# Eight-head edge attention: residual and bias accumulated, centred, in the output product's bank, and a new order of the steps

## The reference, cut to what matters

```
residual = x
q = (x @ Wq + bq).reshape(n, H, HD)
k = (x @ Wk + bk).reshape(n, H, HD)
v = (x @ Wv + bv).reshape(n, H, HD)
score = jnp.einsum('ehd,ehd->eh', q[dst], k[src]) / math.sqrt(HD)
score = score + edge_attr @ We + be
m = jax.ops.segment_max(score, dst, num_segments=n)
exp_s = jnp.exp(score - m[dst])
ssum = jax.ops.segment_sum(exp_s, dst, num_segments=n)
attn = exp_s / (ssum[dst] + 1e-08)
out = jax.ops.segment_sum(attn[..., None] * v[src], dst, num_segments=n)
out = out.reshape(n, D) @ Wo + bo
h = out + residual
mu = h.mean(-1, keepdims=True)
var = ((h - mu) ** 2).mean(-1, keepdims=True)
return (h - mu) / jnp.sqrt(var + 1e-05) * gamma + beta
```

## Time and profile before

| | us |
|---|---|
| median of 3 runs (4201.67 to 4219.3) | 4212.16 |
| the profiled execution | 4234.81 |
| its span | 4233.1 |
| third layer's stage in it | about 2,885 to 3,631 |

### The profile page before, as it was taken

One profiled execution on the slowest core, in us unless ns is written; L12 is line 12 of the kernel. 1 busy time (PEld: TensorE's weight loads), 2 busy tenths in 40 slices (PEclk: granted clock), 3 DMA queues, 4 the chain that ended last, 5 costly groups with the idle time before them and its releaser, 6 DMA issues. The chain is left out here.

```text
span 4233.1 us, 48032 instructions
## 1 busy us (share of the span) xinstructions
PE 2727.4 (64%) x11826; PEld 1768.2 (42%) x11826; DVE 3385.3 (80%) x7569; ACT 2542.3 (60%) x5535; POOL 2439.2 (58%) x2202
## 2 busy tenths in 40 slices
PE   2777877888870588845444553442888787577774
PEld 1555555555550244425433442341444444244442
DVE  2688999999997788837765774883999999699886
ACT  1677777778872366635553562442777777465554
POOL 5455555566630566436636646755566662587777
PEclk7999899999995677756766765565899999566555
DMA  3377567566652888727765764662233332333332
GB/s 87 120 176 182 172 188 193 178 201 193 194 181 74 236 254 254 224 90 225 237 202 167 235 215 140 196 193 74 66 85 85 85 85 60 87 97 97 94 95 68
DMA packets 402066, 644.05 MB, mean 152 GB/s; under 512 B 127455, under 2 KB 207720, under 8 KB 401790
## 3 DMA queue, kind: packets, MB, share of 16 engines
q1 hardware_dynamic: 332030, 527.96, 41.0%
q0 software_dynamic: 69760, 113.02, 11.0%
HBM read 347.78 MB, written 296.81 MB: 152 GB/s over the span
## 5 line engine op out<-in xcount | busy, mean ns | idle before, releaser
L1603 POOL DMA_INDIRECT gs_g<-table_xw,slot_idx x588 | 614.6, 1045 | 454.4 <-issue 250.1
L896 POOL DMA_INDIRECT gs_t<-table_x,slot_idx x392 | 435.1, 1110 | 370.1 <-POOLq L83 144.4
L505 POOL DMA_INDIRECT gs<-x,src_idx x200 | 215.9, 1079 | 406.4 <-DMA xd_rows<-gd 319.6
L378 PE MATMUL ps<-ident,own_g 128*128 128x128 f32 x588 | 145.8, 395 | 466.5 <-DVE own_g L1705 383.3
L1649 ACT ACTIVATE hT_g<-u_g 128x512 f32<-128x512 f32 x147 | 92.5, 630 | 516.5 <-DVE u_g L1717 340.9
L1710 DVE TENSOR_TENSOR_SCAN agg_g<-same_seg,agg_g,ps 128x512 f32<-128x512 uint8 x147 | 187.8, 1278 | 228.7 <-DMA table_x<-x_b 104.3
L1272 POOL DMA_INDIRECT slot_idx<-node_map,src_idx x200 | 239.5, 1198 | 196.6 <-DMA slot_idx<-node_map,src_idx 92.9
L378 PEld LDWEIGHTS ps<-ident,own_g 128*128 128x128 f32 x588 | 97.9, 200 | 507.3 <-DVE own_g L1705 415.9
L505 POOL DMA_INDIRECT gd<-x,dst_idx x200 | 245.2, 1226 | 60.9 <-issue 60.3
L1879 POOL DMA_INDIRECT out<-x_t,end_idx x196 | 232.8, 1188 | 65.0 <-issue 58.8
L896 POOL DMA_INDIRECT own_t<-table_x,own_idx x196 | 225.6, 1151 | 59.7 <-issue 59.7
(11 more groups left out here) (366 smaller groups left out, 9479.7 us busy)
## 6 DMA issues: line engine op xcount, KB each, us to landing
table_xw<-xw_b SPq DMA_DIRECT2D x147, 512.0 KB
table_x<-x_b SPq DMA_DIRECT2D x98, 512.0 KB
own_g<-table_xw SPq DMA_DIRECT2D x147, 256.0 KB
x_in<-x SPq DMA_DIRECT2D x49, 512.0 KB
y_g<-table_x SPq DMA_DIRECT2D x49, 512.0 KB
table_xw<-xw_g SPq DMA_DIRECT2D x98, 256.0 KB
out<-y_g SPq DMA_DIRECT2D x49, 512.0 KB
pen_t<-pen_row SPq DMA_DIRECT2D x98, 256.0 KB
```

The costliest lines, as they stand in the source:

```text
L378: last = nc.tensor.transpose(to[0:width, j * P:(j + 1) * P], t[:, j * width:(j + 1) * width], ident[:])
L505: pool.indirect_dma_start(out=to[k % 3][:, j * D:(j + 1) * D], out_offset=None, in_=x, in_offset=bass.IndirectOffsetOnAxis(ap=of[:, n:n + ...
L896: pool.indirect_dma_start(out=self.B[L % RING][g][:, t * D:(t + 1) * D], out_offset=None, in_=table, in_offset=bass.IndirectOffsetOnAxis(a ...
L1603: pool.indirect_dma_start(out=gs[c % 6][:, j * D:(j + 1) * D], out_offset=None, in_=tables[layer], in_offset=bass.IndirectOffsetOnAxis(ap= ...
```

## The change

The new h is made in PSUM. `copy_xT` adds bo to each column of `xdT` while it copies (`bo_col`), so that `xdT` holds the own rows plus bo, turned. `rows_o` first multiplies those by `centre` (the identity minus 1/128), which turns them back into rows and takes their mean away, and then accumulates the products with Wo on top in the same bank. Wo itself is centred once at the start of the program, so K[7] holds h minus its mean. `xo`, `h_res` and the shift `nm` of the normalisation "d" go. `d.stats` reads K[7] in place of `u`, and `d.apply` reads K[7] and only scales. So K[7] is now held until `d.apply` has finished: `rows_o` of lane L waits for it of lane L-1. As Wq is now multiplied with rows that have bo in them, Wq times bo is taken off bq at the start. All places of the stage's plan are new. The number of table loads stays.

```
-                "load": (1, "ea_in pen_in"), "residual": (129, "xo x2b"),
-                "turn_x": (-37, "xsT_ps xdT_ps"), "copy_xT": (62, "xsT xdT"), "products": (78, "k_ps q_ps"),
...
+                "load": (1, "ea_in pen_in"), "residual": (152, "x2b"),
+                "turn_x": (-58, "xsT_ps xdT_ps"), "copy_xT": (17, "xsT xdT"), "products": (42, "k_ps q_ps"),
...
+                nc.tensor.matmul(ps[:, 5, P:P + 1], Wq[:], bo_col[:], start=True, stop=True).then_inc(S("bo_q_ps"), 1)
...
+                V.tensor_reduce(wo_sum[:], Wo[:], AX.X, ALU.add).then_inc(S("wo_sum"), 1)
+                v.wait_ge(S("wo_sum"), 1)
+                V.scalar_tensor_tensor(out=Wo[:], in0=wo_sum[:, 0:1].to_broadcast([P, D]), scalar=-1.0 / D, in1=Wo[:],
+                                       op0=ALU.mult, op1=ALU.add).then_inc(S("wo_c"), 1)
...
+                V.tensor_tensor(bq[:], bq[:], ps[:, 5, P:P + 1], ALU.subtract)
...
                         @step("rows_o")
                         def _(L):
+                            b = B[L % RING]
+                            step.due(pe, "d_out", L, 1)
+                            step.due(pe, "xdT", L)
+                            for j in range(SUB):
+                                nc.tensor.matmul(K[7][:, j * D:(j + 1) * D], b["xdT"][:, j * P:(j + 1) * P], centre[:],
+                                                 start=j == 0, stop=False, skip_group_check=True)
                             step.due(pe, "oT", L)
-                            step.due(pe, "h_res", L, 1)
-                            rows_times(pe, K[7], B[L % RING]["xsT"], Wo).then_inc(S("wo_ps"), 1)
+                            for j in range(SUB):
+                                last = nc.tensor.matmul(K[7][:, j * D:(j + 1) * D], b["xsT"][:, j * P:(j + 1) * P], Wo[:],
+                                                        start=False, stop=j == SUB - 1, skip_group_check=True)
+                            last.then_inc(S("wo_ps"), 1)
...
-                            nc.scalar.copy(b["xdT"][:], K[1]).then_inc(S("xdT"), 1)
+                            nc.scalar.activation(b["xdT"][:], K[1], ACT.Identity, bias=bo_col[:, 0:1]).then_inc(S("xdT"), 1)
...
+                        @step("d.apply")
+                        def _(L):
+                            b = B[L % RING]
+                            step.due(act, "d_rs", L)
+                            for j in range(SUB):
+                                last = nc.scalar.activation(b["v"][:, j * D:(j + 1) * D], K[7][:, j * D:(j + 1) * D], ACT.Copy, scale=b["rs"][:, j:j + 1])
+                            last.then_inc(S("d_out"), 1)
...
-                            V.tensor_tensor(rows4(b["xo"][:]), rows4(b["own"][:]), each_row(bo), ALU.add).then_inc(S("xo"), 1)
...
+                        @step("d.stats")
+                        def _(L):
+                            ln_stats(v, step, "d", L, B[L % RING], K[7], "wo_ps")
+
+                        @step("d.scale")
                         def _(L):
                             b = B[L % RING]
-                            step.due(v, "wo_ps", L)
-                            step.due(v, "xo", L)
-                            V.tensor_tensor(b["u"][:], K[7], b["xo"][:], ALU.add).then_inc(S("h_res"), 1)
-
-                        ln_vector(v, step, B, "d", "u", "h_res")
+                            step.due(v, "d_sd", L)
+                            nc.vector.reciprocal(b["rs"][:], b["sd"][:]).then_inc(S("d_rs"), 1)
```

More of the change, by code:

```diff
@@ L115, in build @@
     Wq, Wk, Wv, Wo = (sb(n, [P, D]) for n in ("Wq", "Wk", "Wv", "Wo"))
-    bq, bk, bv = (sb(n, [P, 1]) for n in ("bq", "bk", "bv"))
+    bq, bk, bv, bo_col = (sb(n, [P, 1]) for n in ("bq", "bk", "bv", "bo_col"))
     bo, gamma2, beta2 = (sb(n, [P, D]) for n in ("bo", "gamma2", "beta2"))
@@ L157, in build @@
         sums = tb("sums", [P, 6, 4])
-        bo_sum = tb("bo_sum", [P, 1])
+        bo_sum, wo_sum = tb("bo_sum", [P, 1]), tb("wo_sum", [P, 1])
         Win, WinT, Ws0 = tb("Win", [P, D]), tb("WinT", [P, D]), tb("Ws0", [P, D])
@@ L1771, in build @@
             lag, plan = HOP4_LAG, {
-                "load": (1, "ea_in pen_in"), "residual": (129, "xo x2b"),
-                "turn_x": (-37, "xsT_ps xdT_ps"), "copy_xT": (62, "xsT xdT"), "products": (78, "k_ps q_ps"),
-                "values": (173, "v_ps"), "copy_z": (73, "kb"), "qk": (118, "qk"), "scores": (81, "z_ps"),
-                "maximum": (157, "M_first M dz Dm0 Dm"), "gather": (-420, ""), "exps": (172, "p F"),
-                "sums": (192, "msg den num"), "scores_e": (54, ""), "turn_sums": (218, "den_rows"), "divisor": (276, "dn rd"),
-                "widen_rd": (264, "rd_wide"), "turn_rd": (260, "rdT_ps"), "divide": (303, "oT"), "rows_o": (339, "wo_ps"), "h_res": (330, "h_res"),
-                **ln_plan("d", 400, 358, 425, 437), "x3_pre": (437, "dg x3_pre"), **ln_plan("e", 467, 483, 502, 509),
-                "store": (565, "stored"), "turn_q": (581, "x3T_ps"), "copy_q": (632, "x3T"),
-                "query": (648, "q3_ps"), "keep_q": (649, "q_kept"), "store_q": (655, "q_out")}
+                "load": (1, "ea_in pen_in"), "residual": (152, "x2b"),
+                "turn_x": (-58, "xsT_ps xdT_ps"), "copy_xT": (17, "xsT xdT"), "products": (42, "k_ps q_ps"),
+                "values": (126, "v_ps"), "copy_z": (74, "kb"), "qk": (111, "qk"), "scores": (72, "z_ps"),
+                "maximum": (186, "M_first M dz Dm0 Dm"), "gather": (-420, ""), "exps": (156, "p F"),
+                "sums": (224, "msg den num"), "scores_e": (13, ""), "turn_sums": (197, "den_rows"), "divisor": (311, "dn rd"),
+                "widen_rd": (290, "rd_wide"), "turn_rd": (263, "rdT_ps"), "divide": (324, "oT"), "rows_o": (284, "wo_ps"),
+                **ln_plan("d", 343, 359, 397, 370), "x3_pre": (465, "dg x3_pre"), **ln_plan("e", 472, 479, 580, 594),
+                "store": (640, "stored"), "turn_q": (602, "x3T_ps"), "copy_q": (638, "x3T"),
+                "query": (672, "q3_ps"), "keep_q": (695, "q_kept"), "store_q": (700, "q_out")}
         else:
@@ L1790, in build @@
         with ExitStack() as tmp:
-            hop = Line(tmp, f"t{kind}", plan, lag, "xsT pen kb qk p F den num msg xo " + ("xdT w" if kind == 2 else "own u x4"),
+            hop = Line(tmp, f"t{kind}", plan, lag, "xsT pen kb qk p F den num msg " + ("xdT w" if kind == 2 else "xo own u x4"),
                       {"gs": (table, NT + GT, slot_idx), **({"own": (table, NT + GT, own_idx)} if kind == 2 else {})})
@@ L1867, in _ @@
                     def _(L):
-                        for name in ["xsT_ps"] + ["xdT_ps", "xo", "x2b"] * (kind == 2):
+                        for name in ["xsT_ps"] + ["xdT_ps", "x2b"] * (kind == 2):
                             step.due(pool, name, L, RING)
@@ L2034, in _ @@
                             nc.scalar.copy(B[L % RING]["q"][:], K[6][0:4, :]).then_inc(S("q_kept"), 1)
-                        ln_act(act, step, B, "d", "v", "u")
+                        @step("d.root")
+                        def _(L):
+                            ln_root(act, step, "d", L, B[L % RING])
+                        @step("d.apply")
[5 more added lines that the diff above has]
+                            last.then_inc(S("d_out"), 1)
                         ln_act(act, step, B, "e", "xn", "u")
@@ L2130, in _ @@
                             hop.due_gathered(v, L)
-                            V.tensor_tensor(rows4(b["xo"][:]), rows4(b["own"][:]), each_row(bo), ALU.add).then_inc(S("xo"), 1)
                             V.tensor_tensor(rows4(b["w"][:]), rows4(b["own"][:]), each_row(beta2), ALU.add).then_inc(S("x2b"), 1)
-                        @step("h_res")
+                        @step("d.stats")
+                        def _(L):
+                            ln_stats(v, step, "d", L, B[L % RING], K[7], "wo_ps")
+                        @step("d.scale")
                         def _(L):
                             b = B[L % RING]
-                            step.due(v, "wo_ps", L)
-                            step.due(v, "xo", L)
-                            V.tensor_tensor(b["u"][:], K[7], b["xo"][:], ALU.add).then_inc(S("h_res"), 1)
-                        ln_vector(v, step, B, "d", "u", "h_res")
+                            step.due(v, "d_sd", L)
+                            nc.vector.reciprocal(b["rs"][:], b["sd"][:]).then_inc(S("d_rs"), 1)
                         @step("x3_pre")
```

3 lines of the change are left out of this document (2 added, 1 removed).

## The result

The changed kernel takes **4259.3 us** (median of 4 runs, 4258.19 to 4261.95), the kernel before, beside it, 4213.15 (4 runs). The ratio is 1.0121, interval [1.0094, 1.0148]: slower by 46 us, where 32 us less were forecast. The changed kernel's profiled execution took 4261.95 us, that of the kernel before 4234.81: 27 more.

The account below looks back on a forecast made before the run. DVE bound the kernel at 13.38 us a lane; after the change a circle through ACT and PE would, at 12.5 plus 0.2 for the clock. 47 lanes save 32 us: 4212.2 - 32 = 4180, range 4147 to 4222.

Parts of the forecast that it names:

- DVE's own work: DVE's instructions in a lane: `xo`, `h_res` and `nm` go, 0.11 us comes in, 12.0 us if DVE never waits.
- The circle through ACT and PE: From ACT's `kb` to the next lane's `kb`: 12.5 us a lane; as likeliest outcome 4161 to 4191 us, chance 0.50.
- the one from 12.5 to 12.7: Allowance in the lane time for PE's low clock lengthening `scores`, `turn_x` and `query`: 0.2 us a lane.
- the clock: PE's low-clock share halves to 9%, 1.1 us a lane, a third to a half on `scores`, `turn_x`, `query`: 0.2 us.
- Rival D: PE's clock drops on `scores`, `turn_x` and `query` in each lane: 14.2 us a lane, 38 us more, 4250; chance 0.10.
- The argument against D: PE's remaining idle time is 1 to 1.5 us a lane, where it was 3.6.
- C: DVE's `d.stats` and maximum scan wait for PE: 12.93 to 13.8 us a lane, 4191 to 4232 us; chance 0.18.
- The sum: Whole kernel: 47 x (13.38 - 12.7) = 32 us less, start and drain cancelling, giving 4180 us.

Follow-up runs that it names:

- the third chip: Chip that ran the new arithmetic at the old places, alone (3858.98 us, ratio 0.9804 to the kernel before) and with instructions added at the start of the stage's code.
- i1: Changed kernel with a one-row transfer in place of each indirect gather from lane 10 (counted from 0) on: 4147.0 us, ratio 0.9849 to the kernel before.
- e3: Changed kernel with only `query` moved, ahead of the next lane's `turn_x` on PE: 4246.08 us, ratio 0.9979 to the kernel before.
- i2: Changed kernel without the four products with `centre`, all places kept: 4201.03 us, ratio 0.9966 to the kernel before.
- e5: Changed kernel with `d.stats` moved later on DVE, behind the divisor's steps: 4254.63 us, ratio 1.0064 to the kernel before.
- h0: Changed kernel, unaltered, run again on the fourth chip: 4270.02 us, ratio 1.0096 to the kernel before.

## Why the prediction was wrong

- **DVE's own work: right, 0.25 too high.** 12.0 us a lane; 11.75 measured on the third chip with DVE busy throughout. BN_STATS on PSUM 416 ns (median of 70), on SBUF 425 in the same lanes: no cost, so the Trainium skill's 120 fixed cycles for a source in PSUM ("VectorE: DVE Perf Modes", on the TRN2 errata) are again not to be seen.
- **The circle through ACT and PE: right.** 12.5 forecast, 12.2 measured wherever nothing disturbs it (the lane of 12.17, i1 from lane 6 on), and 11.9 where e3 takes `turn_x` out of it. `d.apply` took 1.14 us for four passes (1.1 to 1.3 forecast). At the old places it is shorter and DVE binds, 11.75.
- **The step that failed** is the one from 12.5 to 12.7, in the words "I take half of today's share ... 0.2 us": everything that could hold PE up was priced at 0.2 us a lane. Measured are 1.9 over the undisturbed 12.2, from two things.
- **One is the clock, mis-sized.** The low clock did not halve as PE's idle time shrank: PEclk is 0.92 against 0.91, 2.15 us at the lower level in a lane (2.4 before). Nor does a third to a half of it fall on the circle's steps: 75% falls on `scores`, `turn_x` and `query`. At half speed, 2.15 us can cost at most 1.1 of the 1.9; the 18 lanes without a late result are 1.1 longer than 12.2.
- **The other was put at nothing: late results.** The prediction read PE's rows as completions. The 28 lanes with late results hold some 70 of the 89 us that the 46 lanes take over 12.17 each, part of it by the clock drops in them. They could have been seen: the kernel before has 28 such results. There they cost nothing (13.35 us in lanes with one, 13.52 in the others), which fits its 3.6 us of idle PE in a lane.
- **Rival D's price (14.2 us a lane, 4250 us; measured 14.1 and 4259) was met in part by luck.** Its mechanism, the drop on `scores`, `turn_x` and `query`, is real, and pure in i2: 1.7 forecast, 1.8 measured (13.95 against 12.17). But it comes in some lanes and not in each, and late results, which D does not have, make up the rest. The argument against D was that PE's idle time would be 1 to 1.5 us. It is 1.7 in an undisturbed lane, and it doesn't decide: lanes with the same idle time do and don't have a drop. What does decide stays open.
- **C, waits for PE at `d.stats`: real, but small.** 33.6 us in 10 + 11 waits over 35 lanes, two thirds of it (the `remote` ones) behind late results. e5 brings it from 46 us in h0's window of 500 us to 11 and gains 0.5 us a lane; in its place DVE waits 34 us for `kb`.
- **The sum holds where nothing disturbs**: lanes of 12.2 give 47 x 1.2 = 56 us less, and i1, without gathers from the eleventh lane on, took 66 less than the kernel before with its gathers (4147.0 against 4213.1). Measured are 14.1 to 14.6, so 1.4 to 1.9 more than the 12.7 forecast, against a gain of 0.7. The changed kernel itself was not run on the third chip; by its undisturbed lanes it should take 12.2 there, which is not shown.

The version to keep is the new arithmetic at the old places: ratios 0.9956, 0.9804 and 0.9968 on three chips, against 1.0121, 1.0053 and 1.0096 for the changed kernel.

## What to carry to other kernels

When a change moves the bound from one engine to a circle through several, price the circle with each of its PE steps at the lower clock as well, and let that price, not a share of it, be the bound of a rival with a fair chance: here it was 1.7 us a lane. PE's idle time in an undisturbed lane did not tell which lanes drop. Idle time on an engine that is not the bound costs nothing, but it is what hides late results: before spending it, count the waits whose releaser is "remote" or "issue" behind a PE row that has long ended, and compare when the semaphore rose with when the row ended. And time both halves of a change, the arithmetic and the order, apart and on more than one chip.

## What the runs showed of the hardware

- One and the same kernel took 3934 us on one chip and 4213 to 4255 on four others. On that one, with the new arithmetic at the old places, PE's clock stayed at 1.00 through the stage and no lane was long; the kernel before was not profiled there.
- PE's results can come 2 us and more behind the modelled end while the clock row reads 1.00. In e3 ACT's copies of two groups of four transposes, recorded 0.5 us apart on PE, came 2.2 us apart (a window over it, then ACT's timeline). The view's brackets name a DMA here, wrongly: the semaphores that rose, at 3099.71 and 3101.89, are those of the two groups.

```profile
3096.00:3104.00 8.00, 3.77 (x23) 2.60 (x22) 2.97 (x4) 3.74 (x6) 6.14 (x6) 1.00 0.22 63
```

```profile
3099.73 0.58 ACT L2011 COPY xsT_t<-ps 128x512 f32<-128x512 f32 x1 [2.25 <-DMA out<-y_g]
3101.91 0.69 ACT L2016 ACTIVATE xdT_t<-ps,bo_col 128x512 f32<-128x512 f32 x1 [1.59 <-DMA out<-y_g]
```

From one group of four transposes to the next it is 0.44 us in the rows of the upper clock (3061.95 to 3062.39) and 0.85 in those of the lower (3140.30 to 3141.15), so 2.2 is slower than either. The Trainium skill ("TensorE: Matmul & The Clock Gate", under "Seeing it yourself") warns that the clock's events in a trace have been seen to be unreliable and the gate to be stuck at a quarter. By the two distances a quarter would give about 1.7 (an estimate), so the 2.2 are no proof of it; that late results are low clock which the record lacks is a rival that no run here settles.

- Every lane of more than 18 us, in whatever profile, is the 11th, 22nd, 33rd or 44th, whatever the lane's mean length (13.3 to 14.6 us in those profiles), so these follow the program and not the time; what in it, the shifts of code did not find. Not each of the four is long in each profile (the first profile of the changed kernel has only 11 and 22), and lanes of 16 to 17.6 also lie elsewhere.
